# Weight loads and a zeroed tile moved from the attention stage into the preparation, and a wait on keys split in two

## What is computed

```python
h = layernorm(x) * (1 + ca) + sa
q, k, v = split(h @ qkv_w + qkv_b)              # 16 heads of width 8
q_prime = relu(einsum('bhld,hdm->bhlm', q, proj))   # 64 features per head
k_prime = relu(einsum('bhld,hdm->bhlm', k, proj))
kv_cumsum = cumsum(k_prime (x) v)               # causal: a running state per head
context = einsum('bhlm,bhlmd->bhld', q_prime, kv_cumsum)
norm = einsum('bhlm,bhlm->bhl', q_prime, cumsum(k_prime))
x = x + ga * (context / (norm + 1e-6) @ out_w + out_b)
```

## Time and profile before

| | us |
|---|---|
| median of three runs | 971.23 (969.6 to 971.88) |
| the profiled execution: its own time | 972.43 |
| its span, first to last instruction | 970.6 |
| TensorE busy in the span | 808.2 |
| VectorE busy | 733.8 |
| ScalarE busy | 441.3 |
| POOL busy | 209.3 |

### The profile page before, as it was taken

One profiled execution on the slowest core, in us unless ns is written; L12 is line 12 of the kernel. 1 busy time (PEld: TensorE's weight loads), 2 busy tenths in 40 slices (PEclk: granted clock), 3 DMA queues, 4 the chain that ended last, 5 costly groups with the idle time before them and its releaser, 6 DMA issues. The chain is left out here.

```text
span 970.6 us, 26710 instructions
## 1 busy us (share of the span) xinstructions
PE 808.2 (83%) x10846; PEld 458.1 (47%) x10846; DVE 733.8 (76%) x1384; ACT 441.3 (45%) x785; POOL 209.3 (22%) x174
## 2 busy tenths in 40 slices
PE   7477999988898746889987969999996887689895
PEld 4255767666676512334433423433332664345452
DVE  3535445888999969999887866888885457599985
ACT  3654655756655515556687822111112255423232
POOL 4233000100100120000007743333331000124330
PEclk9799999999998967999998999999998899899998
DMA  5051000000000003556739498888882000000001
GB/s 134 15 116 47 5 5 4 4 4 5 4 4 3 4 1 126 232 234 265 262 150 358 177 335 281 283 272 266 261 271 84 1 1 1 1 11 12 22 11 33
DMA packets 49700, 104.43 MB, mean 108 GB/s; under 512 B 9968, under 2 KB 24112, under 8 KB 49456
## 3 DMA queue, kind: packets, MB, share of 16 engines
q1 hardware_dynamic: 45360, 100.68, 29.9%
q10 hardware_dynamic: 4224, 2.10, 0.8%
HBM read 53.48 MB, written 48.23 MB: 105 GB/s over the span
## 5 line engine op out<-in xcount | busy, mean ns | idle before, releaser
L1299 PE MATMUL bank<-RS,Wd 128*128 128x512 f32 x256 | 132.0, 604 | 10.2 <-DVE RS L1362 9.9
L1362 DVE TENSOR_TENSOR RS<-so_ug,bank 128x512 f32<-128x512 f32 x128 | 84.0, 672 | 24.3 <-PE bank L1285 13.2
L965 ACT ACTIVATE att_qk<-bank 128x512 f32<-128x512 f32 x128 | 66.8, 601 | 61.8 <-PE bank L736 61.8
L1264 POOL TENSOR_TENSOR so_ug<-so_ug 128x512 f32<-128x512 f32 x48 | 62.3, 1298 | 110.2 <-DMA so_ug<-hidden 110.2
L1299 PEld LDWEIGHTS bank<-RS,Wd 128*128 128x128 f32 x256 | 46.6, 190 | 61.8 <-DVE RS L1362 31.5
L1605 POOL TENSOR_TENSOR so_made<-so_ug 128x512 f32<-128x512 f32 x23 | 35.6, 1565 | 160.1 <-DVE bank L1808 150.3
L1629 ACT ACTIVATE so_ug<-bank,bu 128x512 f32<-128x512 f32 x80 | 54.7, 684 | 18.5 <-PE bank L57 18.4
L55 PE MATMUL bank<-Hhi,Wgh 128*128 128x512 f16 x128 | 49.3, 386 | 8.8 <-DVE so_made L1760 8.5
L1976 POOL TENSOR_TENSOR ff_xn_h<-ff_xn_h,la_qT 128x1408 f32<-128x1408 f32 x7 | 22.2, 3170 | 153.6 <-DVE ff_xn_h L99 153.6
L1060 DVE TENSOR_TENSOR att_am<-bank,causal 128x512 f32<-128x512 f32 x32 | 22.0, 688 | 38.3 <-PE bank L773 38.3
L454 DVE TENSOR_TENSOR att_sorting<-att_sorting 128x256 f32<-128x256 f32 x103 | 49.9, 485 | 0.0
(11 more groups left out here) (421 smaller groups left out, 1911.3 us busy)
## 6 DMA issues: line engine op xcount, KB each, us to landing
so_ug<-hidden SPq DMA_DIRECT2D x48, 768.0 KB, 4.5
hidden<-so_off SPq DMA_DIRECT2D x48, 512.0 KB, 2.9
hidden<-so_made SPq DMA_DIRECT2D x80, 256.0 KB, 2.0
so_ug<-hidden SPq DMA_DIRECT2D x16, 512.0 KB, 4.1
prep_xin<-in_L_attn_x_dram ACTq DMA_DIRECT2D x8, 256.0 KB, 7.8
out_dram<-ff_ot SPq DMA_DIRECT2D x8, 256.0 KB, 2.2
so_other<-so_key SPq DMA_DIRECT2D x2, 512.0 KB, 5.6
prep_wm<-in_L_wmod_dram SPq DMA_DIRECT2D x2, 384.0 KB, 5.8
```

The lines of the kernel that those rows point to most:

```text
L965: nc.scalar.activation(qk[t % 2][:, r, :, :].rearrange("p a l -> p (a l)"), psF[r], ACT.Relu).then_inc(s_["fe"], 1)
L1264: nc.gpsimd.tensor_tensor(u, u, g, ALU.mult).then_inc(s_pp, 1)
L1299: nc.tensor.matmul(psY[j][:, :], Wd[:, n, :], hh[n % 4][:], start=False, stop=n == EBLK - 1).then_inc(s_dn[n % 4], 1)
L1362: nc.vector.tensor_tensor(hh[i][:], pg[four % 2][:, i if four % 2 else i // 2 * 3 + i % 2, :], psW[k % 4][:, :], ALU.mult).then_inc(s_hh[k ...
```

## The change

Three things. First, twelve of the fourteen loads behind the zeroed fp4 tile are issued in the preparation, as soon as the last tile of x has landed and the fp4 tile is zeroed; `bdown`'s two stay and go behind `br`. POOL's conversions in attention then wait once, for `Wr` and `bdown` and for the moved `Wup` group. Second, the zeroing of `v1` and of the fp4 tile goes to the end of POOL's list in the preparation; `v1` becomes a tile that lives from the preparation to the end of attention, and five semaphores live as long. Third, the state product waits for the first half of the keys ahead of its first matmul, and for the second half ahead of the pair of heads p = 4, the 17th matmul of 32.

```diff
+        ahead = ExitStack()
+        s_ahead = {n: ctx.enter_context(nc.semaphore("ahead_" + n)) for n in ("wzero", "preset", "wq", "ew", "wg")}
+        n_ahead = dict.fromkeys(("wq", "ew", "wg"), 16)
+        v1 = ahead.enter_context(nc.sbuf_tensor("v1", [P, 2, 2, 4, NH, 32], F32))
+        wq_n, wu_f, wg_f = RS[:, 0:QW], keys[:], F2f[:]
...
                     load("wo", Wo0[:], out_w[:, :])
+
+                    def load_ahead(which, dst, src):
+                        sp.dma_start(dst, src).then_inc(s_ahead[which], 16)
+                        n_ahead[which] += 16
+                    sp.wait_ge(s_x[NU - 1], 32)
+                    sp.wait_ge(s_ahead["wzero"], FIRST + 1)
+                    for i, w in enumerate((w_gate, w_up)):
+                        for k, n in enumerate(NBLK):
+                            load_ahead("wq", wq_n[0:n, (3 * i + k) * P:(3 * i + k + 1) * P], w[P * k:P * k + n, :])
+                    load_ahead("wq", wq_n[:, 6 * P:QW], w_down[:, :])
+                    load_ahead("ew", wu_f.rearrange("p (e h) -> p e h", h=HH), Wup.rearrange("e d h -> d e h"))
+                    load_ahead("ew", bg[:], bgate.rearrange("(k a) h -> (a h) k", a=4))
+                    load_ahead("wg", wg_f.rearrange("p (e h) -> p e h", h=HH), Wgate.rearrange("e d h -> d e h"))
+                    load_ahead("wg", Wd[:], Wdown.rearrange("(k a) h d -> (a h) k d", a=4))
+                    load_ahead("wg", bu[:], bup.rearrange("(k a) h -> (a h) k", a=4))
                     sp.wait_ge(s_["wo"], 16 + n_load["wo"])
...
                     assert step.n == N_CONST
+                    nc.gpsimd.memset(wq_n, 0.0).then_inc(s_ahead["wzero"], 1)
+                    step = Chain(pool, s_ahead["preset"], first=FIRST)
+                    step(nc.gpsimd.memset(v1[:], 0.0))
+                    for j in range(2):
+                        rows = slice(P // 2 * j, P // 2 * j + P // 2)
+                        step(nc.gpsimd.memset(v1[rows, :, j, :, :, HD:HD + 1], 1.0))
...
-                        for n, (hi, lo), src in (("wr", Wrs, wr_f[:]), ("ew", bd, bd_f[:]), ("ew", Wu, wu_f)):
-                            pool.wait_ge(s_load[n], n_load[n])
+                        pool.wait_ge(s_load["wr"], n_load["wr"])
+                        pool.wait_ge(s_ahead["ew"], n_ahead["ew"])
+                        for (hi, lo), src in ((Wrs, wr_f[:]), (bd, bd_f[:]), (Wu, wu_f)):
...
                         def state(t):
-                            pe.wait_ge(*keys_out(t + 1))
                             pe.wait_ge(s_["vd"], FIRST + 2 * (t // 4) + 2)
                             for p in range(NH // 2):
+                                if p % 4 == 0:
+                                    pe.wait_ge(s_["kte"], FIRST + 2 * t + p // 4 + 1)
...
         causal_attention()
+        ahead.close()
         route()
```

More of the change, by code:

```diff
@@ L131, in sb, with scoped, stand @@
             return ctx.enter_context(nc.sbuf_tensor(name, shape, dt))
-        def scoped(stage):
+        def scoped(stage, kept=()):
             taken = []
-            def stand(dma=()):
+            def stand(dma=(), ahead=()):
                 engines = (nc.sync, nc.scalar, nc.vector, nc.gpsimd)
-                for i, h in enumerate(taken):
+                for i, h in enumerate(taken + list(ahead)):
                     engines[i % len(engines)].sem_inc(h, 16 if h in dma else FIRST)
@@ L144, in clear @@
             def clear():
-                nums = sorted(h.num for h in taken)
+                nums = sorted(h.num for h in taken + list(kept))
                 runs = [n for n in nums if n - 1 not in nums]
@@ L232, in cols @@
                 return slice(u * ST, (u + 1) * ST)
-            stand(dma=[s_[n] for n in n_load] + s_x)
+            stand(dma=[s_[n] for n in n_load] + s_x + [s_ahead[n] for n in n_ahead], ahead=s_ahead.values())
             with nc.allow_non_contiguous_dma("small transposed weights"), nc.Block() as block:
@@ L607, in causal_attention @@
             with ExitStack() as tmp:
-                sem, stand = scoped(tmp)
+                sem, stand = scoped(tmp, kept=s_ahead.values())
                 def tb(name, shape):
@@ L630, in causal_attention @@
                 wr_f, bd_f, w1_f, wo1_f = tb("wr_f", [P, E]), tb("bd_f", [P, P]), tb("w1_f", [P, 3, P]), tb("wo1_f", [P, P])
-                wu_f, wg_f = keys[:], F2f[:]
-                wq_n, wq_q = RS[:, 0:QW], RS[:, 3 * 256:3 * 256 + QW]
+                wq_q = RS[:, 3 * 256:3 * 256 + QW]
                 work = {"xn": tb("wq_xn", [P, QW]), "m": sorting, "tiny": tiny}
                 work |= {k: tb("wq_" + k, [P, QW // 16]) for k in ("sc", "rc")}
-                names = ("preset", "f", "fe", "kt", "kte", "S0", "S1", "Sv0", "Sv1", "Ae", "Ao", "me", "mo", "O", "Od", "To", "den",
+                names = ("f", "fe", "kt", "kte", "S0", "S1", "Sv0", "Sv1", "Ae", "Ao", "me", "mo", "O", "Od", "To", "den",
                          "rd", "o2", "C", "cd", "Y", "yd", "xu", "qk", "qke", "v", "vd", "sort0", "sort1", "sort2",
-                         "mg", "wzero", "gates", "w1T", "w1", "wq", "wqd", "gu", "dn", "pw")
+                         "mg", "gates", "w1T", "w1", "wq", "wqd", "gu", "dn", "pw")
                 s_ = {n: sem("att_" + n) for n in names}
-                s_load = {n: sem("att_load_" + n) for n in ("w1", "wq", "ew", "wg", "wr")}
+                s_load = {n: sem("att_load_" + n) for n in ("w1", "wr")}
                 n_load = dict.fromkeys(s_load, 16)
@@ L669, in _ @@
                         load("wr", brb[:], br[:].partition_broadcast(P))
[L670 to L676, removed]
                         for part in range(2):
[L678 to L681, removed]
+                            load("wr", bd_f[E * part:E * part + E, :], bdown[:, :])
                         for n in s_load:
@@ L1043, in values @@
                             if s == 0:
-                                dve.wait_ge(s_["preset"], FIRST + 3)
+                                dve.wait_ge(s_ahead["preset"], FIRST + 3)
                             if s > 1:
@@ L1137, in weights @@
                             if t == 2:
-                                dve.wait_ge(s_load["wq"], n_load["wq"])
+                                dve.wait_ge(s_ahead["wq"], n_ahead["wq"])
                                 prepare(fp4_scales(nc, prepare, wq_n, n, work))
@@ L1150, in weights @@
                             if t == 9:
-                                dve.wait_ge(s_load["wg"], n_load["wg"])
+                                dve.wait_ge(s_ahead["wg"], n_ahead["wg"])
                                 prepare(nc.vector.tensor_scalar(Wg[0][:], wg_f, WS, None, ALU.mult))
```

1 line of the change is left out of this document (removed).

## The result

| | us |
|---|---|
| before, median of 20 runs | 974.68 (967.65 to 981.14) |
| changed, median of 20 runs | 969.03 |
| ratio of the two | 0.9954, 95% interval 0.9933 to 0.9976 |
| changed, the profiled execution: time, span | 975.05, 973.3 |

The lowest of the changed kernel's runs is 962.15 us; one was disturbed and took 1988.97, and the ratio leaves it out. By the ratio the change makes the kernel faster by 0.46%, 4.5 us of 974.68 (the two medians themselves lie 5.6 us apart); the prediction said 5.6. The point, 965.6, is 3.4 us under the measured median, and as much lies in its start: the median of three runs of before, 971.23, is 3.4 us under that of twenty. So the total looks well forecast. It is not: the stages show a large loss that the prediction put at nothing, and a gain larger than it forecast.

A forecast was written before the change was run, and what follows sets the result against it. The prediction took TensorE's instruction fetch, slowed by weight loads on the DMA engines, to bound early attention. Loads -3.6 and wait by halves -2.0 summed to -5.6 us, from 971.23 to 965.6 us; range 961.5 to 969.5.

The forecast's parts named there:

- The zeroed tile moves ... worth 0: Start of attention: moving POOL's 6.92 us memset into its idle time in the preparation gains 0, since keys finish later.
- Preparation's last Hlo at 40.6: End of the preparation: a sign of being right, VectorE's last Hlo ends at 40.6 us as before.
- In exchange POOL scales and splits Wup right at the start of attention, beside VectorE's first chunks: Start of attention: POOL's Wup work, 12.16 us in the trace, moves earlier and is covered, VectorE having less to do.
- No stall of TensorE there was for VectorE: Attention, 59.98 to 79.75 us: while POOL worked on Wup, TensorE never stalled for VectorE, busy 9.48 of 19.77 us.
- If that cover fails, one chunk comes later by a POOL instruction at the worst: First chunks of attention: the worst cost of POOL's earlier Wup work is one chunk delayed by one POOL instruction.
- The loads, -3.6 us: Attention: without loads, four TensorE instruction pages take 16.1 us instead of 19.77; bounds 0 and -9.9 us; preparation cost 0.
- The last sign of being wrong: Whole kernel: stage and end move apart, so that what attention wins by 184 us is gone by 343 us.
- The wait by halves, -2.0 us: State product in attention: splitting 19 waits for keys, 6.8 us, saves at most 4.3 us, of which 2.0 counted.
- A: Attention: instruction fetches are slow for their own reason, only the wait by halves pays; 969.2 us, chance 0.15.
- B: Attention: the wait by halves gives nothing, TensorE waiting elsewhere; loads alone give 967.6 us, chance 0.17.
- C: Attention: most stalls go, 8 of the 9.9 us and 3 of the halves; 960.2 us, chance 0.10.
- D: Preparation: slower, SP's load issues run past its end and all engines wait at the barrier; chance 0.03.

The follow-up runs named there:

- memset_back: The changed kernel with the zeroing of v1 put back at the start of attention; 963.52 us, ratio to before 0.9866.
- pieces: The changed kernel with the zeroing of v1, still in the preparation, cut into eight chained memsets; 961.86 us, ratio to before 0.9882.
- memset_only: The kernel before with only the zeroing of v1 moved into the preparation, all loads staying in attention; 975.66 us, ratio 0.9989.
- loads_only: As memset_back, but the state product waits for both halves of the keys as before; 968.46 us, ratio to before 0.9918.
- gates_early: The kernel before with VectorE's gate arithmetic moved from chunk 1 to chunk 0, loads staying; 973.66 us, ratio 0.9985.
- late_gate: The kernel before with the last three loads (Wgate, Wdown, bup) held back until the end of chunk 4; 974.82 us in one run.
- halves_only: The kernel before with only the state product's wait for the keys split by halves; 971.58 us, ratio 0.9950.
- before_again: The kernel before, unchanged, profiled a second time; 977.9 us.
- lock_back: memset_back with POOL's conversion of Wup held until the end of chunk 0, to meet VectorE's gate arithmetic; 965.35 us, ratio to before 0.9919.
- pieces_full: As pieces, but the state product waits for both halves of the keys as before; 967.84 us, ratio to before 0.9943.
- gated: The changed kernel with POOL's zeroing of v1 held until VectorE's silu product is out; 963.56 us in one run.

## Why the prediction was right and wrong

**"The zeroed tile moves ... worth 0": the step that failed.** Its half on attention held: with the memset there (`memset_back`) the kernel is no slower than without (`pieces`). But the step said that POOL's 6.92 us go "to the preparation, into its idle time", and asked only what POOL had free, not who works beside it. VectorE was held for 3.9 us there, TensorE's clock was low behind it, and the preparation ended 5.4 and 7.1 us later than in the two profiles of before; by the times it cost 8.6 us in place of 0 on top of the other two changes. On top of the kernel before it cost nothing that can be measured (`memset_only`); why its clock was low for so much shorter stays open. "Preparation's last Hlo at 40.6" was the test named in the prediction, and it failed at 46.02.

**"In exchange POOL scales and splits Wup right at the start of attention, beside VectorE's first chunks": right for the changed kernel, for a wrong reason.** "No stall of TensorE there was for VectorE" was true of one profiled execution, in which two instruction lists had missed each other by 3 us. In the next one TensorE waited 5.46 us. "If that cover fails, one chunk comes later by a POOL instruction at the worst" is just what happens, in the kernel before: both profiles of the changed kernel are without it, and the prediction did not count that as a gain.

**The loads, -3.6 us: right in mechanism, too small by the times.** Pages of 3.7 to 4.1 us without loads; preparation's cost 0, as forecast: SP was done at 33.9 us, for which 36.7 had been estimated, and the preparation of `loads_only` ends at 39.08. The four pages took 14.7 to 16.3 us without loads; the forecast 16.1 was inside that, though it was taken from the next four, which take 15.4 to 16.8 us without loads. So against the first profile of before the changed kernel gains 4.8 us there, and its second profile against the second of before, with the hold in it, 8.2. By the times `loads_only` measures 8.0 us (4.7 to 11.3), inside the bound of 9.9; what this has beyond the fetch, 3.4 to 5.1 us, is in part the hold that its profile no longer has, at most 4.5 us on average by `gates_early`. The last sign of being wrong did not come: between 184 and 343 us nothing of the gain was lost (the window of 158.68 us holds 4562 matmuls in the changed kernel, 4489 before).

**The wait by halves, -2.0 us: right by the traces** (-2.2), in number of waits as well (18 to 21 gone, 19 forecast).

**The rivals.** A, that pages are slow for their own reason, is refuted by `late_gate`, where slow pages followed the loads, and by `loads_only`, which gains 4.7 us or more. B, that the halves give nothing, is refuted by `halves_only` (upper end 0.9984). C, that most stalls go, is not what happened: stalls up to 1.50 us remain. D placed the loss in the preparation, but by SP's issues; SP was 12 us ahead of VectorE. The loss in the preparation came from POOL, for which the prediction had no rival.

**The sum.** Forecast -3.6 - 2.0 + 0 = -5.6; measured by the kernels -8.0 - 4.9 + 8.6 = -4.3 with -4.5 for the whole. The 8.6 is itself taken from the whole, so this sum is no test of it; the tests are the 7.5 us of the preparation and `pieces`, which is worth -11.5 us of 972 where the whole change is worth -4.5. The forecast came out near by luck: the missed gain, 7.3 us, and the missed loss, 8.6, are nearly of one size.

**Better than both kernels** are `memset_back` (0.9866) and `pieces` (0.9882): the change without its one bad move. `pieces` against `memset_back` can't be told apart; they have 5 and 6 runs.

## What to carry to other kernels

Idle time of POOL is not free for work on SBUF: look up what VectorE does from SBUF to SBUF in that stretch, and who waits for it; where the work must be there, cut the POOL instruction, since only the piece that is running holds the other engine. And where two engines' lists slide against each other, one profiled execution shows one of several alignments: profile the kernel before a second time before costing a stretch at nothing.

## What the runs showed of the hardware

- Not every VectorE instruction is held. During the 6.93 us memset an addition of 128x8 from SBUF to SBUF was (4.02 us in place of 0.16), a product of a PSUM and an SBUF operand was not (0.69 us at 16.98, beside it). Beside POOL's instructions that read SBUF, `SCALAR_TENSOR_TENSOR` on 128x8 was held as well (1.74 and 3.91 us in place of 0.17). The same section of the Trainium skill's page on SBUF draws this line: an instruction of VectorE with two inputs in SBUF is locked out only by one of POOL that reads SBUF. The trace agrees with its 1.74 and 3.91 us, and on the other side with `pieces`, where a product with both inputs in SBUF took its usual time while a memset ran:

```profile
17.95 0.17 DVE L443 TENSOR_TENSOR prep_cT<-prep_cT,prep_ce 128x8 f32<-128x8 f32 x1
```

- The fetch of TensorE's instructions under load: single pages of 5.1 to 5.8 us and others of 3.8 to 4.7 (7.24 us for the one before 64.24 us in `before_again`, of which 3.01 us is the stall and a part passed at half the clock); 3.7 to 4.1 us on average over four pages without loads.
- TensorE's clock at the start of attention is mostly one of two things. From its first matmul there to the start of the last page ahead of the four it took 12.5 to 13.3 us in seven profiles (before, `gates_early`, `late_gate`, `memset_back`, `lock_back`, `pieces`, `pieces_full`) and 15.4 to 15.5 in six (`before_again`, `halves_only`, `loads_only`, `memset_only`, both of the changed kernel), where the clock goes to half a second time, for 10.2 us; `gated` lies between, 14.3 us with 3.4 us at half. All four profiles with the whole memset in the preparation are among the slow ones or `gated`, and three of the ten others are. Whether the hold brings it about, or chance, stays open; it is 3 us of the spread between single profiles and may be part of the 8.6.
